# A decoder layer on one core: softmax sums as products of their own in the first group, one feed-forward tick moved in front of the output projection

## The chip, the cores and the metric

One core of a Trainium2 chip runs the whole program. The metric is the device time in microseconds (us), taken as the median of the runs shown. The engines are named as the profile names them: PE is TensorE (PEld its weight loads), DVE is VectorE, ACT is ScalarE, POOL is GpSimd, SP is the engine that issues most transfers.

## What is computed

The reference is one decoder layer over x (16 sequences of 128 tokens, 256 channels, fp32) and a context of 64 channels per token:

```
x = x + attn(layernorm(x))            # linear attention, 32 heads of 8, head norm, silu gate, Wo
x = x + xattn(layernorm(x), ctx)      # causal softmax attention, 16 heads of 16, Wout
x = x + ffn(layernorm(x))             # 8 experts (top 2), 176 hidden each, and a shared one of 704
```

The change touches the end of the second line, for each head

```
scores = q @ k.T / sqrt(16)           # causal mask
out    = softmax(scores) @ v          # = (exp(s - max) @ v) / sum(exp(s - max))
x      = x + out @ Wout.T
```

and the place of the work of the third line among that of the next group of sequences.

## The kernel before, in words

The 16 sequences go in four groups of four (g = 0 to 3; the title's "first group" is g = 0). A group goes through linear attention, then cross attention, then the output projection `Wout`, the residual and the third layer norm, and the router. Its feed-forward part is not done then: it is cut into 36 ticks (17 blocks of 128 hidden rows for each half of the tokens, and two to drain) and runs between the steps of the next group. The feed-forward of group 3 runs alone at the end.

A tick n is spread over the engines. PE makes the gate and up products of block n (L1018 to L1020, 12 matmuls of 256 columns, or 6 for the last block of a half, which has 64 rows) and the down products of block n - 2 (L1056 to L1058, 6 matmuls). ACT takes the silu (L774), DVE multiplies gate by up (L1469), POOL multiplies by the routing weight (L616), ACT makes the rounded high part (L764), POOL the low part (L605); the down products wait for that low part (`h_lo`). `COUNT` says how many ticks stand at which named point of a group's program: n0 to n5 up to the query projection, x0a to x3c in cross attention (b = 0 to 3 is the sequence), y0 in front of the output projection, r0 to r3 behind it. Every engine has its instructions in a fixed order written out by hand, and semaphores between engines.

Cross attention of a sequence b: scores and row maxima (DVE L1571), transposed exponentials (ACT L881), the causal cut (POOL L670), and `attend` (L1266): 16 matmuls that give, for 32 columns per head, 16 columns of values and 16 of ones, that is outputs and sums side by side. For one half of the heads the sums lie on the partitions on which the other half has its values, so ACT copies the bank twice with masks (`first_heads`, L890 and L891), DVE adds the other half (`second_heads`, L1584 and L1585), and then `attended` takes the reciprocal (L1590), swaps partitions within pairs (L1592) and multiplies (L1595), which releases `yT_ready`. Group 0 has two sets of score banks and runs two sequences at a time; matmuls on constants (`idle_product`, L988) stand between its `attend` calls. The output projection (`out_projection`, L1196) is in two halves, for sequences 0 and 1 and for 2 and 3; the second waits for the `yT_ready` of sequence 3. Then DVE adds the residual (L1638), takes the statistics, POOL the root (L548), DVE applies it (L1385), and PE turns the result (`turn_norm`, L979).

In the shadow of that the next group begins: its first layer norm is turned by PE (L979), copied by ACT (`mixed_input`, L724) and DVE (`input_differences`, L1411 to L1415); both copies wait for POOL to zero the edge column (`zero_edge`, L556). DVE mixes the inputs (L1423), and PE projects them (`project`, L1014).

## Time and profile before

| | us |
|---|---|
| median of 3 runs | 668.2 (667.42 to 668.63) |
| the profiled execution | 670.88 |
| its span, first to last instruction | 668.8 |
| PE busy in the span | 615.7 (92%) |
| DVE busy | 409.9 (61%) |
| POOL busy | 338.4 (51%) |
| ACT busy | 280.6 (42%) |
| mean granted clock of TensorE | 0.977 |

The profile has a page (busy time, waits, the chain that ended last) and the trace behind it can be asked for a stretch. The granted clock is a share of 2.4 GHz; 0.5 is its lower level, 1.2 GHz. PE is the engine that is nearly always busy, so the places where it stands idle, or runs at the lower clock, are what is to be read.

### The profile page before, as it was taken

The numbers are of one execution on the slowest core, as the hardware profiler recorded it, in microseconds if no ns is written. First come the engines' busy times: TensorE is split into PE (matmuls) and PEld (weight loads), VectorE is DVE, ScalarE is ACT, GpSimd is POOL, SyncE is SP. The second block draws the span as 40 slices with busy tenths as digits, with TensorE's granted clock in tenths as the row PEclk, the third lists the DMA queues.
The fourth block names the chain that finished last, engine by engine and source line by source line (L and its number), as shares of the span: only waits on it lengthen the run. The fifth ranks groups of instructions, "written<-read, shape, count | busy, mean of one in ns | idle before, by whom it ended". The sixth has DMA issues, their size and how long they took to land.

```text
span 668.8 us, 15291 instructions
## 1 busy us (share of the span) xinstructions
PE 615.7 (92%) x6184; PEld 486.1 (73%) x6184; DVE 409.9 (61%) x856; ACT 280.6 (42%) x640; POOL 338.4 (51%) x453
## 2 busy tenths in 40 slices
PE   7987978499999999799999999899999999999996
PEld 6444446354888889654797888764697889889996
DVE  6797789759643555778763555768863365652220
ACT  4956234042335655242324655233323666343332
POOL 6673155014355666324364765333364666518766
PEclk9989987699999999899999999899999999999999
DMA  8921000002031121002021111002011111104220
GB/s 191 355 61 33 1 1 2 0 1 65 26 84 28 39 62 42 14 16 66 11 84 42 38 56 41 21 16 65 10 48 35 43 44 60 22 27 132 69 70 17
DMA packets 41824, 34.08 MB, mean 51 GB/s; under 512 B 9901, under 2 KB 41206, under 8 KB 41754
## 3 DMA queue, kind: packets, MB, share of 16 engines
q1 hardware_dynamic: 39850, 31.27, 16.9%
q10 hardware_dynamic: 1904, 1.84, 0.8%
q8 instruction: 49, 0.80, 0.5%
q14 instruction: 21, 0.17, 0.1%
HBM read 30.92 MB, written 2.17 MB: 49 GB/s over the span
## 4 chain that ended last, share of the span: by engine, by line
PE 33%; DVE 25%; POOL 17%; ACT 11%; issue 11%; DMA 2%; ACTq 0%; POOLq 0%; DVEq 0%
PE bank L1014 6%; DVE A L1494 6%; DVE nm L1571 5%; POOL hb L616 5%; POOL A L691 3%; POOL hT_last L700 3%; POOL hT L605 3%; PE bank L1196 3%; PE bank L1123 2%; ACT A L881 2%; ACT L795 2%; PE bank L1112 2%; PE bank L1011 2%; PE bank L1213 2%; DVE hb L1469 2%
## 5 line engine op out<-in xcount | busy, mean ns | idle before, releaser
L605 POOL TENSOR_TENSOR hT<-hb,hT 128x256 fp32r<-128x256 f32 (+1 forms) x102 | 78.4, 769 | 75.6 <-ACT hT L764 75.6
L616 POOL TENSOR_TENSOR hb<-hb,cwb 128x256 f32<-128x256 f32 (+1 forms) x102 | 76.4, 749 | 75.5 <-DVE hb L1469 75.4
L1469 DVE TENSOR_TENSOR hb<-hb,bank 128x256 f32<-128x256 f32 (+1 forms) x102 | 42.7, 419 | 115.3 <-ACT hb L774 115.3
L764 ACT ACTIVATE hT<-hb 128x256 fp32r<-128x256 f32 (+1 forms) x102 | 42.4, 416 | 128.5 <-POOL hb L616 128.5
L1018 PE MATMUL bank<-xTf,wGh 128*128 128x256 f32 x272 | 83.4, 307 | 0.0
L1494 DVE TENSOR_TENSOR A<-bank,decay 128x512 f32<-128x512 f32 x128 | 77.5, 681 | 8.4 <-PE bank L1112 8.4
L1019 PE MATMUL bank<-xTf,wGh 128*128 128x256 f32 x272 | 76.7, 282 | 0.0
L1020 PE MATMUL bank<-xTf,wGl 128*128 128x256 f32 x272 | 76.6, 282 | 0.0
L1019 PE MATMUL bank<-xTf,wUh 128*128 128x256 f32 x256 | 72.2, 282 | 0.0
L1018 PE MATMUL bank<-xTf,wUh 128*128 128x256 f32 x256 | 72.1, 282 | 0.0
L1020 PE MATMUL bank<-xTf,wUl 128*128 128x256 f32 x256 | 72.1, 281 | 0.0
L570 POOL TENSOR_TENSOR A<-A,mcol 128x512 f32<-128x512 f32 x32 | 35.1, 1101 | 71.6 <-PE bank L1112 64.6
L1056 PE MATMUL bank<-wDh,hT 128*128 128x256 f32 (+1 forms) x204 | 59.8, 293 | 5.3 <-POOL hT L605 4.9
L1018 PEld LDWEIGHTS bank<-xTf,wGh 128*128 128x128 f32 x272 | 51.5, 189 | 8.9 <-issue 6.2
L1058 PE MATMUL bank<-wDh,hT 128*128 128x256 f32 (+1 forms) x204 | 57.1, 280 | 0.0
L1057 PE MATMUL bank<-wDl,hT 128*128 128x256 f32 (+1 forms) x204 | 57.1, 280 | 0.0
L774 ACT ACTIVATE hb<-bank 128x256 f32<-128x256 f32 (+1 forms) x102 | 38.1, 374 | 44.3 <-PE bank L1020 44.2
L1019 PEld LDWEIGHTS bank<-xTf,wGh 128*128 128x128 f32 x272 | 51.4, 189 | 0.2
L1020 PEld LDWEIGHTS bank<-xTf,wGl 128*128 128x128 f32 x272 | 51.2, 188 | 0.0
L1571 DVE TENSOR_REDUCE nm<-bank 128x16 f32<-128x2048 f32 x16 | 36.5, 2283 | 19.7 <-PE bank L1234 19.5
L1018 PEld LDWEIGHTS bank<-xTf,wUh 128*128 128x128 f32 x256 | 48.3, 189 | 0.0
L1019 PEld LDWEIGHTS bank<-xTf,wUh 128*128 128x128 f32 x256 | 48.2, 188 | 0.0
(217 smaller groups left out, 1436.2 us busy)
## 6 DMA issues: line engine op xcount, KB each, us to landing
cwb<-cw_rows SPq DMA_DIRECT2D x54, 128.0 KB, 3.0
A<-cw_rows SPq DMA_DIRECT2D x18, 128.0 KB, 3.2
A<-in_x SPq DMA_DIRECT2D x4, 512.0 KB, 4.2
res<-in_x SPq DMA_DIRECT2D x4, 512.0 KB, 4.3
out_x<-res SPq DMA_DIRECT2D x8, 256.0 KB, 2.4
rawG<-in_L_ffn_w_gate SPq DMA_DIRECT2D x2, 704.0 KB, 6.2
rawU<-in_L_ffn_w_up SPq DMA_DIRECT2D x2, 704.0 KB, 6.8
cwb<-cw_rows SPq DMA_DIRECT2D x12, 112.0 KB, 2.5
```

What stands on the lines that cost most here:

```text
L605: pool.tensor_tensor(hT[hr, c % 2, 1, :], hb[hr, c % 2, :], hT[hr, c % 2, 0, :].bitcast(F32), ALU.subtract).then_inc(h_lo, 1)
L616: pool.tensor_tensor(hb[hr, c % 2, :], hb[hr, c % 2, :], cwb[hr, c % CWS, :], ALU.mult).then_inc(h_scaled, 1)
L764: act.activation(hT[hidden(n), c % 2, 0, :], hb[hidden(n), c % 2, :], ACT.Copy).then_inc(h_hi, 1)
L1018: mm(out_ap, wh, xh, start=start, stop=False, skip_group_check=skip)
L1019: mm(out_ap, wh, xl, start=False, stop=False, skip_group_check=skip)
L1020: return mm(out_ap, wl, xh, start=False, stop=stop, skip_group_check=skip)
L1056: mm(o, hi[:, t], wDh[hr, j, :], start=(j == 0 and b == 0), stop=False, skip_group_check=True)
L1057: mm(o, hi[:, t], wDl[hr, j, :], start=False, stop=False, skip_group_check=True)
L1058: last = mm(o, lo[:, t], wDh[hr, j, :], start=False, stop=j == FB - 1, skip_group_check=True)
L1469: tt(h, h, up_part(PS[5 + c % 2], n), ALU.mult).then_inc(gu_used, 1)
L1494: tt(att[:, (u % 2) * 4 + i, :].rearrange("p (j t) -> p j t", j=4), PS[SCORE_BANKS[(4 * u + i) % 7]][:, :].rearrange("p (j t) -> p j t", j=4),
L1571: nc.vector.tensor_reduce(nm[:].rearrange("p (i h) -> p i h", i=4), PSB[:, score_base(g, b):score_base(g, b) + 4, :].rearrange("p i (h t) ...
```

## The change

In group 0 the kernel goes back to sums that are products of their own: `attend` there makes 32 matmuls of which 16 have a constant of ones and zeros (`onesp`, made by three more POOL instructions at the start) as weights, the halves of heads accumulate in one bank, and DVE's `attended` is a reciprocal read from the bank and a multiplication. ACT's copies, the two DVE additions, the swap and the `idle_product` calls between the `attend` calls go. The next group's first turn, its copy and its differences come after the last `attend` of group 0, the output projection of group 0 waits for all four sequences, and two of DVE's splittings of weights move from x2a to r2.

In groups 1 to 3 the arithmetic of `attend` is as before. `zero_edge` moves in front of the x3c ticks. One tick leaves n4 (2 to 1) and one is added at y0 (1 to 2), so that every tick from n5 to x3c is one number lower. On DVE the first y0 product stands in front of the normalisation of sequence 3 (`normalised`, the former `attended`) and the second behind it. `project(g + 1, 0)` moves in front of the down products of r2, and `mixed_input(g + 1, 1)` in front of r1 on DVE.

```diff
+        onesp = sb("onesp", [P, 2, 2 * XD], F32)
...
-        COUNT = dict(n0=1, n1=2, n2=2, n3=2, n4=2, n5=1, y0=1, r0=2, r1=1, r2=1, r3=1)
+        COUNT = dict(n0=1, n1=2, n2=2, n3=2, n4=1, n5=1, y0=2, r0=2, r1=1, r2=1, r3=1)
...
-        LOW_AT = dict(n5=(1, 2, 3), x0a=(0, 4, 5), x2a=(6, 7))
+        LOW_AT = dict(n5=(1, 2, 3), x0a=(0, 4, 5), r2=(6, 7))
...
+            made(pool.memset(onesp[:], 0.0))
+            for w in range(2):
+                made(pool.memset(onesp[:, w, XD * w:XD * w + XD], 1.0))
...
+                    if b == GB - 1 and g + 1 < NG:
+                        zero_edge(g + 1)
                     point(g, f"x{b}c")
 
-                if g + 1 < NG:
-                    zero_edge(g + 1)
                 point(g, "y0")
...
                         point(g, f"x{b}b")
-                        first_heads(b)
-                        if b == 2:
-                            mixed_input(1)
-                        first_heads(b + 1)
...
+                if g == 0:
+                    mixed_input(1)
                 point(g, "y0")
...
                     for m in range(2):
+                        for s in range(2):
+                            for w in range(2):
+                                for i in range(4):
+                                    v = xvp[:, b, 8 * m + 2 * i + w, :] if s == 0 else onesp[:, w, :]
+                                    a = (2 * s + m) * T
+                                    last = mm(PS[attend_bank(g, b)][32 * i:32 * i + 32, a:a + T], v, weights_of(g, b)[:, i, (2 * m + w) * T:(2 * m + w + 1) * T],
+                                              start=w == 0, stop=w == 1, skip_group_check=True)
...
                         attend(b)
-                        if b == 2:
-                            turn_norm(0, 1, tokx, 2)
-                        idle_product(10 - 2 * b, 1)
                         attend(b + 1)
...
+                if g == 0:
+                    turn_norm(0, 1, tokx, 2)
                 point(g, "y0")
-                if g == 0:
-                    pe.wait_ge(o_taken, 3)
-                out_projection(yT, [(yT_ready, g * 4 + 2), (yT_ready, g * 4 + 2)], wX[:, 1], (0, 1), wout_ready)
+                halves = 2 if g else 4
+                out_projection(yT, [(yT_ready, g * 4 + halves), (yT_ready, g * 4 + halves)], wX[:, 1], (0, 1), wout_ready)
...
                     down(g - 1, n - 2)
+                if g + 1 < NG:
+                    project(g + 1, 0)
                 point(g, "r2")
                 if g + 1 < NG:
-                    project(g + 1, 0)
                     point(g, "r3")
...
+                def attended(b):
+                    dve.wait_ge(o_part, g * 4 + b + 1)
+                    if b:
+                        dve.wait_ge(yT_ready, g * 4 + b)
+                    nc.vector.reciprocal(rec, PS[attend_bank(g, b)][:, 2 * P:4 * P]).then_inc(rec_ready, 1)
+                    dve.wait_ge(rec_ready, g * 4 + b + 1)
+                    tt(yT[:, :, b * T:(b + 1) * T], PS[attend_bank(g, b)][:, 0:2 * P].rearrange("p (m t) -> p m t", m=KC),
+                       rec.rearrange("p (m t) -> p m t", m=KC), ALU.mult).then_inc(yT_ready, 1)
...
-                point(g, "y0")
+                if g:
+                    ffn_tick(g - 1, ticks_at(g, "y0")[0])
+                    normalised(GB - 1)
+                    for n in ticks_at(g, "y0")[1:]:
+                        ffn_tick(g - 1, n)
+                else:
+                    input_differences(1)
...
+                if g + 1 < NG:
+                    mixed_input(g + 1, 1)
                 point(g, "r1")
                 if g + 1 < NG:
-                    for c in range(1, 4):
+                    for c in range(2, 4):
                         mixed_input(g + 1, c)
```

DVE before, at the end of group 1's cross attention: the last sequence's additions, reciprocal, swap and product, then the y0 tick's product (hb is the hidden block, A the activations) and the residual.

```order
L1584 SCALAR_TENSOR_TENSOR S<-bank,xcol,S 128x256 [waits o_copied]
L1585 SCALAR_TENSOR_TENSOR A<-bank,xcol,A 128x2x128
L1590 RECIPROCAL S<-S 128x256 [waits sums_ready]
L1592 STREAM_SHUFFLE S<-S 128x256 [waits rec_ready]
L1595 TENSOR_TENSOR A<-A,S 128x2x128 [waits o_taken,rec_swapped]
L1469 TENSOR_TENSOR hb<-hb,bank 128x256 [waits silu_done]
L1638 TENSOR_TENSOR res<-bank,res 128x512 [waits wout_ready]
```

DVE in the changed kernel, at the same place.

```order
L1603 SCALAR_TENSOR_TENSOR S<-bank,xcol,S 128x256 [waits o_copied]
L1604 SCALAR_TENSOR_TENSOR A<-bank,xcol,A 128x2x128
L1479 TENSOR_TENSOR hb<-hb,bank 128x256 [waits silu_done]
L1609 RECIPROCAL S<-S 128x256 [waits sums_ready]
L1611 STREAM_SHUFFLE S<-S 128x256 [waits rec_ready]
L1614 TENSOR_TENSOR A<-A,S 128x2x128 [waits o_taken,rec_swapped]
L1479 TENSOR_TENSOR hb<-hb,bank 128x256 [waits silu_done]
L1656 TENSOR_TENSOR res<-bank,res 128x512 [waits wout_ready]
```

One product of a tick now stands ahead of the reciprocal and the other behind the swap and the multiplication.

PE before, behind the turn of group 1's third norm: the end of the down products of r1, those of r2, the first projection of group 2 and the first of r3.

```order
L1056 MATMUL bank<-wDh,hT 128x256 [waits h_lo]
L1057 MATMUL bank<-wDl,hT 128x256
L1058 MATMUL bank<-wDh,hT 128x256
L1056 MATMUL bank<-wDh,hT 128x256
L1057 MATMUL bank<-wDl,hT 128x256
L1058 MATMUL bank<-wDh,hT 128x256
L1014 MATMUL bank<-A,wA 128x512 [waits xm_ready,o_taken]
L1014 MATMUL bank<-A,wA 128x512 [waits xm_ready] x3
L1056 MATMUL bank<-wDh,hT 128x256 [waits h_lo]
```

The six ahead of the projection here are those of r2. PE in the changed kernel, at the same place.

```order
L1057 MATMUL bank<-wDl,hT 128x256
L1058 MATMUL bank<-wDh,hT 128x256
L1014 MATMUL bank<-A,wA 128x512 [waits xm_ready,o_taken]
L1014 MATMUL bank<-A,wA 128x512 [waits xm_ready] x3
L1056 MATMUL bank<-wDh,hT 128x256 [waits h_lo]
L1057 MATMUL bank<-wDl,hT 128x256
L1058 MATMUL bank<-wDh,hT 128x256
L1056 MATMUL bank<-wDh,hT 128x256
L1057 MATMUL bank<-wDl,hT 128x256
L1058 MATMUL bank<-wDh,hT 128x256
L1056 MATMUL bank<-wDh,hT 128x256 [waits h_lo]
```

Now the projection follows the down products of r1, and those of r2 and r3 stand together behind it.

PE before, in group 0, at the first two `attend` calls (pexB holds the second sequence's exponentials).

```order
L1266 MATMUL bank<-A 32x128 x15
L988 MATMUL bank<-identb 128x512 x10
L1266 MATMUL bank<-pexB,A 32x128 [waits p_ready]
L1266 MATMUL bank<-pexB,A 32x128 x15
L1227 MATMUL bank<-maskS,identb 128x512 [waits o_taken,p_exp]
```

PE in the changed kernel, at the second of them.

```order
L1277 MATMUL bank<-A,onesp 32x128 x8
L1277 MATMUL bank<-pexB,A 32x128 [waits p_ready]
L1277 MATMUL bank<-pexB,A 32x128 x7
L1277 MATMUL bank<-pexB,onesp 32x128 x8
L1277 MATMUL bank<-pexB,A 32x128 x8
L1277 MATMUL bank<-pexB,onesp 32x128 x8
L1227 MATMUL bank<-maskS,identb 128x512 [waits yT_ready,p_exp]
```

The ten matmuls on constants are gone, 16 matmuls are added to each call, and the next scores wait for DVE's last product of the sequence before instead of its last addition.

## Rows read from the trace of the kernel before

**Rows 1.** The page: busy time of PE and the granted clock in 40 slices
```profile
PE 615.7 (92%) x6184; PEld 486.1 (73%) x6184; DVE 409.9 (61%) x856; ACT 280.6 (42%) x640; POOL 338.4 (51%) x453
...
PEclk9989987699999999899999999899999999999999
```
**Rows 2.** What PE waited for: us in total, times, longest
```profile
PE bank L1196 <- DVE A L1595: 11.8, 4, 4.9
```
**Rows 3.** Timeline of PE, end of groups 1, 2 and 3: start, us, instruction, idle before
```profile
272.71 3.68 PE L1196 MATMUL bank<-wX,A 128*128 128x256 f32 x8 [2.95 <-DVE A L1595]
...
426.64 3.57 PE L1196 MATMUL bank<-wX,A 128*128 128x256 f32 x8 [2.95 <-DVE A L1595]
...
576.50 1.99 PE L1196 MATMUL bank<-wX,A 128*128 128x256 f32 x8 [0.99 <-DVE A L1595]
```
**Rows 4.** Stretches there and of the last feed-forward: length, busy PE to POOL, clock
```profile
269.00:272.70 3.70, 0.76 (x4) 0.33 (x2) 3.62 (x8) 0.26 (x1) 0.80 (x1) 1.00 0.06 15
272.70:276.00 3.30, 3.29 (x9) 2.64 (x9) 1.89 (x6) 0.42 (x1) 1.45 (x2) 0.52 0.08 22
...
576.00:579.00 3.00, 2.50 (x14) 2.29 (x15) 2.82 (x8) 0.42 (x1) 1.47 (x2) 1.00 0.06 6
...
610.00:620.00 10.00, 10.00 (x87) 10.00 (x86) 2.11 (x5) 3.44 (x10) 8.61 (x14) 1.00 0.35 105
```
**Rows 5.** Timeline of DVE at the end of group 1's cross attention
```profile
267.36 0.69 DVE L1411 COPY A<-bank 128x512 f32<-128x512 f32 x1 [0.97 <-POOL A L556]
...
269.98 1.74 DVE L1590 RECIPROCAL S<-S 128x256 f32<-128x256 f32 x1
...
272.23 0.42 DVE L1595 TENSOR_TENSOR A<-A,S 128x256 f32<-128x256 f32 x1
272.57 0.41 DVE L1469 TENSOR_TENSOR hb<-hb,bank 128x256 f32<-128x256 f32 x1
```
**Rows 6.** One line's instructions: duration in ns, least, median, most
```profile
L1595 DVE TENSOR_TENSOR A<-A,S x14: 425/866/881, 96.3 to 576.0; 128x256 f32<-128x256 f32 x14
```
**Rows 7.** Timeline around n4 of group 1: second norm applied, turned
```profile
191.19 1.80 DVE L1385 TENSOR_SCALAR A<-res,mv,rstd 128x256 f32<-128x256 f32 x4
194.68 1.03 PE L979 MATMUL bank<-ident,A 128*128 128x128 f32 x8
```
**Rows 8.** Timeline behind the third norm of group 1, PE and POOL
```profile
281.22 1.04 PE L979 MATMUL bank<-ident,A 128*128 128x128 f32 x8
284.18 0.39 PE L1056 MATMUL bank<-wDh,hT 128*128 128x256 f32 x1 [1.21 <-POOL hT L605]
284.99 3.60 PE L1014 MATMUL bank<-A,wA 128*128 128x512 f32 x8
...
285.82 1.27 POOL L605 TENSOR_TENSOR hT<-hb,hT 64x256 fp32r<-64x256 f32 x1 [0.53 <-ACT hT L764]
```
**Rows 9.** Timeline of group 0's cross attention, PE, POOL and DVE
```profile
89.42 1.08 PE L1266 MATMUL bank<-A 128*32 128x128 f32 x32 [0.43 <-POOL A L670]
...
95.08 1.73 PE L1266 MATMUL bank<-pexB,A 128*32 128x128 f32 x32 [2.31 <-POOL pexB L670]
...
108.67 1.93 PE L1266 MATMUL bank<-A 128*32 128x128 f32 x32
...
109.44 3.30 POOL L670 TENSOR_SCALAR_AFFINE_SELECT pexB<-pexB 128x512 f32<-128x512 f32 x4 [1.35 <-ACT pexB L881]
...
121.64 3.78 PE L1196 MATMUL bank<-wX,A 128*128 128x256 f32 x8 [4.88 <-DVE A L1595]
...
125.45 0.69 DVE L1638 TENSOR_TENSOR res<-bank,res 128x512 f32<-128x512 f32 x1 [2.20 <-PE bank L1196]
```
**Rows 10.** A stretch of group 0, columns as in rows 4
```profile
95.00:99.00 4.00, 3.92 (x44) 2.13 (x48) 2.54 (x6) 0.84 (x2) 1.28 (x2) 0.57 0.00 0
```
**Rows 11.** Timeline of DVE in group 0: two splittings at x2a; idle at r2
```profile
110.86 2.15 DVE L1479 TENSOR_TENSOR wDl<-rawD,wDh 128x768 fp32r<-128x768 f32 x2
...
135.69 1.63 DVE L1423 SCALAR_TENSOR_TENSOR A<-A,cols 128x512 f32<-128x512 f32 x1 [2.15 <-PE bank L1014]
```

More of the change, by code:

```diff
@@ L150, in attend_bank, with attend_released @@
             return score_base(g, b) if g == 0 else 4
-        def sums_of(g, b):
-            return hb[:, 0, :] if g == 0 and b % 2 else rec
         SWAP = list(range(XD, 2 * XD)) + list(range(XD))
+        def attend_released(g, b):
+            return (o_taken, (g - 1) * 4 + b) if g else (yT_ready, b)
         tok2 = A[:, 5120:6144].rearrange("p (b c) -> p b c", b=GB)
```

71 lines of the change are left out of this document (33 added, 38 removed).

## The prediction

> **What bounds the kernel now.** I read the page first. PE is busy for 92% of the span and is at its full granted clock in nearly every slice [rows 1], so time can only come from the places where PE waits or runs at the lower clock. Next the list of what PE waited for: the longest entry is the output projection of cross attention, which waits for DVE's last multiplication (L1595) once per group, 11.8 us in four waits [rows 2]. Then the timeline at those four places. In groups 1 and 2 the second half of that projection waits 2.95 us, in group 3 it waits 0.99 us [rows 3], in group 0 4.88 us [rows 9]. The reader should see a second loss beside the wait: the same 8 matmul records take 3.68 and 3.57 us in groups 1 and 2 but 1.99 us in group 3 [rows 3]. The granted clock says why: in group 1 it is 1.00 over the wait and 0.52 over the 3.30 us behind it, that is nearly all at 1.2 GHz, while in group 3 after a wait of 0.99 us it is still 1.00 [rows 4]. PE's last piece is a wait of 1.21 us for POOL's low part behind the turn of the third norm [rows 8]; it stands in groups 1, 2 and 3 alike. Elsewhere in groups 1 to 3 PE has no wait that the change touches.
>
> **One more tick at y0, one less at n4.** PE's work is the same, only its place changes. A tick is 18 matmuls; over a stretch in which PE does nothing else 87 of them take 10.00 us, 0.115 us each [rows 4], so a tick is 2.07 us. In group 1 PE runs dry at 272.71 - 2.95 = 269.76; with a second tick ahead it does so at 271.83 on the clock of before. What it waits for is DVE's multiplication, which ends at 272.23 + 0.42 = 272.65 [rows 5]. Two edits move that end. The product of the y0 tick now stands in front of the reciprocal: plus 0.41. The edge column is zeroed before the x3c ticks and no longer after them: DVE's copy of the next group's turned input waited 0.97 us for it [rows 5], and everything behind on DVE, the reciprocal of 1.74 us too, comes 0.97 us earlier. So the end is at 272.65 - 0.97 + 0.41 = 272.09 and PE waits 0.26 us. The multiplication took from 0.425 to 0.881 us over its 14 records [rows 6], here 0.42; with POOL now busier beside it it may take 0.45 more, which makes 0.71 us. I take 0.4, between the two. If the edge brings nothing the wait is 1.2 to 1.7 us.
>
> With a wait of 0.4 us I expect no drop of the clock, because 0.99 us left it at 1.00 [rows 4]. Group 1 then saves 2.95 - 0.4 = 2.55 and 3.68 - 1.99 = 1.69, together 4.24 us; group 2 saves 2.55 and 3.57 - 1.99 = 1.58, together 4.13 us; group 3, whose wait of 0.99 is shorter than a tick, saves 0.99 us. **Sum 9.4 us.**
>
> DVE's order at this place puts the reciprocal behind a wait for ACT's silu of the y0 tick; who waits behind it is PE's second half. ACT makes that silu right after the copies that release DVE's additions, so I cost the wait at nothing beyond the 0.41.
>
> The multiplication's two lengths have a rule in the Trainium skill, in SBUF — State Buffer, § Who interferes with whom: a DVE instruction with two SBUF inputs contends with a GpSimd instruction that reads SBUF. By that rule the longer value holds wherever POOL works beside it, and the waits of groups 1 and 2 would be 0.71 us, which makes the sum 0.6 us smaller; by the row taken alone (0.42 at this place) it would be 0.3 us larger.
>
> The tick taken from n4 was cover for the second norm. DVE has applied it at 191.19 + 1.80 = 192.99; PE turned it from 194.68 on [rows 7]. One tick earlier is 192.61, with the last of four sequences needed some 0.77 us later, at 193.38. That is 0.39 us after it is there, so the removal costs nothing; if DVE is late by more than that, PE loses the difference, at most 2.07 us per group. The other ticks, with their 64-row block, their residual addition and SP's transfers of routing rows and of the next x, become one number lower at each point; the engines pass them on in the same rhythm, so I cost that at 0, with a bound of 0.3 us per group either way.
>
> **Down products of r2 behind the projection.** PE waits 1.21 us for the low part [rows 8] and then projects for 3.60 us; in the new order the projection comes first and hides the wait. That is in groups 1 and 2; in group 3 there is no next group and the wait stays. What is late next is the low part of the last block: POOL ends it at 285.82 + 1.27 = 287.09, 5.87 us after the turn began. PE reaches it after the turn and the down products of r1 (282.97, or 1.75 us after that beginning), 3.60 us of projection and 6 matmuls of 0.115, that is at 6.04 us, so it is there by 0.2 us. **2 x 1.21 = 2.4 us**, with 0 as the other bound. The projection needs the second mixed input, which DVE now makes ahead of r1 where it would wait for ACT.
>
> **Group 0.** Each `attend` doubles. The second one ran while the clock was low (95 to 99 us: 0.57 [rows 10]) and took 1.73 us [rows 9], so what follows comes up to 1.73 us later; the scores behind it run partly at the recovered clock and I take 1.5. The ten products on constants had ended 2.31 us before that call and give nothing back. The last `attend` could start when POOL's cut was done, 109.44 + 3.30 = 112.74 [rows 9]; now at 114.24. It takes 2 x 1.08 = 2.16 at the full clock (116.4). DVE's chain behind it is one reciprocal of 1.74 and one multiplication of 0.42, and 0.1 for the handing over (118.7): ACT's copies, the additions, the swap and the three steps of input differences are no longer in it. A reciprocal from a bank is not in the trace; the multiplication's spread bounds what it may add, 0 to 0.45. Then both halves of the projection, 2 x 1.99 less their overlap, 3.9 us: 122.6 against 125.45 before, when DVE added the second half [rows 9]. **Gain 2.9 us.** Bounds: if the first shift does not reach the end, 4.4; if PE stays at the lower clock throughout (no filler products keep it busy now, 1.93 us per 16 matmuls as in one row of rows 9, the projection 2 x 3.78), the end is at 114.24 + 3.86 + 2.26 + 7.56 = 127.9, a loss of 2.5. I take the full clock because PE's work there becomes denser, not sparser. The two splittings, 2.15 us, leave x2a and fall at r2 into an idle stretch of DVE of 2.15 us [rows 11]: 0, or at most a few tenths. The three memsets at the start lie ahead of a root for which POOL waits: 0.
>
> **Sum.** 9.4 + 2.4 + 2.9 = 14.7 us. The profiled execution took 670.88 (span 668.8 and 2.1 around it) and would take 656.2, span 654.1. The median of the runs shown is 668.2, 2.7 below that execution, and the prediction is made for it: 668.2 - 14.7 = **653.5 us**.
>
> **Rivals.**
> 1. Group 0 falls to the lower clock once its fillers are gone. For it: the clock was low there in one stretch even with them [rows 10]. Against: 32 matmuls per call. Time 653.5 + 2.9 + 2.5 = 658.9. Chance 0.12.
> 2. The wait at r2 only moves to the last low part at r3, for which I have 0.2 us: 653.5 + 2.4 = 655.9. Chance 0.08.
> 3. The cover at n4 is missed: DVE's second norm comes late by a tick in three groups. 653.5 + 3 x 2.07 = 659.7. Against: 0.39 us of slack on the row. Chance 0.06.
> 4. The added tick does not cover: its own down products or the silu in front of the reciprocal wait, PE still stands over 1.7 us in groups 1 and 2 and the clock falls as before. 653.5 + 2 x (1.3 + 1.6) = 659.3. This is also the case in which the change does not do what it says. Chance 0.06.
> 5. Slower than before: after the sparse end of group 0 the clock does not come back, and the projections of group 1's inputs, four of 3.60 us, run at 1.2 GHz. That adds 14.4 to rival 1: 673.3. It decides if PE's work from the turn of the third norm on does not lift the clock, which it did before. Chance 0.03.
>
> **How the numbers follow.** The forecast, 651 to 656, has 0.62. The rest, 0.03, is what I don't see. The best sum is 4.4 + 9.4 + 0.8 + 2.4 = 17.0, or 651.2; I set the low end at 650.8. The high end has to take in rivals 1 to 4, so 660.0; rival 5, and two of them at once, are left out, about 0.12. A measurement of this kernel can tell about 0.2% from no change, 1.3 us. Faster has all cases but rival 5 and what I don't see: 0.94; same 0.02; slower 0.04.
>
> **What the changed profile would show.** In groups 1 and 2 two ticks ahead of the output projection, its second half without a wait over 1 us and about 2 us long, the granted clock there 1.00. No wait of PE behind the r1 down products of groups 1 and 2, and one of 1.21 still in group 3. No wait at the turn of the second norm. Group 0's second addition of the residual near 122.6 us instead of 125.45. It would be wrong if the clock at y0 still reads near 0.5, or if the gap reappears at n4 or r3.

## The result and the profile after

The changed kernel takes **650.7 us** (median of 4 runs, 649.97 to 653.28) against 668.4 us (4 runs, 667.42 to 670.11) for the kernel before: ratio **0.9734**, 95% interval 0.9703 to 0.9766. The forecast was 653.5 us with a range of 650.8 to 660.0. The gain is 17.7 us where 14.7 were worked out, so the measured time lies 0.1 us below the low end of the range.

The profiled execution of the changed kernel has a span of 651.6 us, that of before 668.8. The first rows to read are again PE's busy share and the granted clock of the page, which answer to [rows 1]:

```profile
PE 608.5 (93%) x6296; PEld 484.9 (74%) x6296; DVE 409.7 (63%) x840; ACT 277.4 (43%) x632; POOL 337.5 (52%) x456
...
PEclk9989998799999999999999999999999999999999
```

PE has 112 instructions more (128 for the sums of group 0, less the 16 products on constants between its attends) and is busy for 7.2 us less. The slices with an 8 in the middle of the row, one behind each output projection of groups 1 and 2, are gone; only group 0 still shows lower ones.

The list of what PE waited for, to be set against [rows 2]:

```profile
PE bank L979 <- DVE A L1395: 4.0, 1, 4.0
PE bank L1277 <- POOL pexB L674: 3.7, 1, 3.7
PE bank L1056 <- POOL hT L609: 3.0, 8, 1.2
...
PE bank L1196 <- DVE A L1597: 1.7, 1, 1.7
...
PE bank L1196 <- DVE A L1614: 0.4, 2, 0.2
```

The entry of 11.8 us in four waits has become 1.7 us in group 0 and twice 0.2 in groups 1 and 2. The two longest that are left, 4.0 and 3.7 us, are both in group 0, where no feed-forward of a group ahead fills PE.

PE's timeline at the output projection of groups 1, 2 and 3 answers to [rows 3]:

```profile
263.99 1.89 PE L1196 MATMUL bank<-wX,A 128*128 128x256 f32 x8
266.09 1.99 PE L1196 MATMUL bank<-wX,A 128*128 128x256 f32 x8 [0.21 <-DVE A L1614]
...
413.97 1.99 PE L1196 MATMUL bank<-wX,A 128*128 128x256 f32 x8 [0.21 <-DVE A L1614]
...
557.88 3.62 PE L1196 MATMUL bank<-wX,A 128*128 128x256 f32 x16
```

The second half waits 0.21 us where it waited 2.95, takes 1.99 us where it took 3.68 and 3.57, and in group 3 both halves run in one piece. The stretches of group 1 (length, busy time of PE, PEld, DVE, ACT and POOL, granted clock, DMA share, GB/s), as in [rows 4]:

```profile
266.00:268.10 2.10, 2.01 (x10) 1.80 (x11) 1.97 (x7) 0.42 (x1) 1.12 (x2) 1.00 0.10 29
268.10:271.40 3.30, 3.30 (x30) 3.30 (x30) 3.03 (x9) 0.39 (x1) 1.57 (x3) 1.00 0.07 22
```

The clock is 1.00 (2.4 GHz) where it was 0.52, which is 1.2 GHz nearly throughout. DVE there, as in [rows 5]:

```profile
260.26 0.68 DVE L1421 COPY A<-bank 128x512 f32<-128x512 f32 x1
...
263.03 0.40 DVE L1479 TENSOR_TENSOR hb<-hb,bank 128x256 f32<-128x256 f32 x1
263.36 1.74 DVE L1609 RECIPROCAL S<-S 128x256 f32<-128x256 f32 x1
...
265.61 0.42 DVE L1614 TENSOR_TENSOR A<-A,S 128x256 f32<-128x256 f32 x1
```

The copy that waited 0.97 us for the edge waits for nothing, the y0 tick's product stands in front of the reciprocal, and the last multiplication takes 0.42 us. PE behind the third norm of group 1, as in [rows 8]:

```profile
272.92 1.04 PE L979 MATMUL bank<-ident,A 128*128 128x128 f32 x8
...
274.51 3.60 PE L1014 MATMUL bank<-A,wA 128*128 128x512 f32 x8
...
279.65 1.06 PE L1330 MATMUL bank<-xTf,wR 128*10 128x128 f32 x32
```

No wait stands between the turn and the router's product (L1330, which is L1320 before); the one of 1.21 us is gone in groups 1 and 2, and group 3 still has it, at 569.29.

**Where the time came from.** The start of the router's product marks each group well, since nothing but group 0 differs ahead of the first. It stood at 135.58, 289.41, 443.24 and 587.64 us and stands at 131.62, 279.65, 427.52 and 570.65. Cut further at the first half of the output projection and at the turn of the third norm, the 17.2 us between the two spans divide so:

| stretch | forecast | measured |
|---|---|---|
| group 0, up to its router product | 2.9 | 3.96 |
| projection to third norm's turn: groups 1, 2, 3 | 4.24, 4.13, 0.99 | 4.42, 4.31, 1.26 |
| turn to router product: groups 1, 2 | 1.21, 1.21 | 1.46, 1.47 |
| all else (cover at n4, shifted ticks, tail) | 0 | 0.3 |
| sum | 14.7 | 17.2 |

**A second thing is needed to read the times.** The profiled execution of the changed kernel is 3.3 us above the lowest of the other three. The further kernels below point to the reason: their profiled executions differ in the granted clock of the first 40 us, and in nearly all of them group 0 goes with it (start of the router product of group 0, us):

| clock of 0:40 | group 0 as before | group 0 as changed | gain |
|---|---|---|---|
| 1.00 | 132.96 and 132.97 (fill_gap, rest_only) | 128.44 to 128.50 (tick_back, order_back, split_back) | 4.5 |
| 0.97 | 135.58 (before) | 131.62, 131.46, 131.41 (after, edge_back, proj_back) | 4.0 to 4.2 |
| 0.91, 0.92 | none | 134.18, 134.37 (after_again, g0_only) | |

The mean over those 40 us isn't the whole of it. fill_norm below, whose only edit lies behind the output projection of group 0, starts that projection at 116.95 with a clock of 0.92; after_again does so at 120.01 with 0.91, and the changed kernel at 117.05 with 0.97. Two kernels below that edit the new group 0 itself, g0_fillers and pow_late, have their router products at 128.77 and 129.15 with a clock of 1.00.

Behind that product two executions of the changed kernel agree to 0.1 us (519.98 and 519.92 us from there to the end). The forecast took 2.7 us off the profiled execution for the median. A likely cause lies here: the profile of before is of the second row, while most of the timed executions of both kernels have times that fit the first. Only one execution of each kernel is profiled, so this isn't shown. Row against row the gain is 4.5 + 13.2 = 17.7 us, which is what the medians say.

### The profile page after: what moved, and what is told of

Same layout as the page of the kernel before. It is cut to its first block, busy times and chain, and to the rows that moved or that the text cites. A ratio compares the mean times of both kernels' runs of the same rounds, so it can differ in the third digit from the quotient of the medians.

```text
span 651.6 us, 15490 instructions
## 1 busy us (share of the span) xinstructions
PE 608.5 (93%) x6296; PEld 484.9 (74%) x6296; DVE 409.7 (63%) x840; ACT 277.4 (43%) x632; POOL 337.5 (52%) x456
## 3 DMA queue, kind: packets, MB, share of 16 engines
q1 hardware_dynamic: 39850, 31.27, 17.2%
## 4 chain that ended last, share of the span: by engine, by line
PE 36%; DVE 23%; POOL 17%; ACT 11%; issue 10%; DMA 2%; ACTq 0%; SPq 0%; POOLq 0%; DVEq 0%
PE bank L1014 7%; DVE A L1504 6%; DVE nm L1581 5%; POOL hb L620 4%; POOL A L695 3%; POOL hT_last L704 3%; PE bank L1196 3%; POOL hT L609 3%; ACT A L885 2%; PE bank L1123 2%; ACT L799 2%; PE bank L1011 2%; PE bank L1213 2%; PE bank L1112 2%; DVE hb L1479 2%
```

## The experiments

Medians therefore move by up to 3 us with the mixture of starts. I read each kernel by its **steps**, from one router product to the next in its profiled execution (before 153.83, 153.83, 144.40 and a tail of 81.16; after 148.03, 147.87, 143.13, 80.95), and give the times beside them. In tick_back and proj_back the tail, which no edit touches, is 3.0 us longer, and in order_back 1.2 us (82.15). It is left out of the steps, but the times have it. The difference is the clock's. In all 16 profiled executions PE waits about 1.2 us and then 0.2 to 0.4 us around the router product of group 3; in these three it then runs at 1.2 GHz for 3 to 7 us (proj_back 0.50 to 0.51 from 574 to 580 us), in the other thirteen the product runs at the full clock. The same product in proj_back and in the changed kernel:

```profile
573.07 1.89 PE L1329 MATMUL bank<-xTf,wR 128*10 128x128 f32 x32 [0.39 <-DVE xTf L1672]
```

```profile
570.65 1.06 PE L1330 MATMUL bank<-xTf,wR 128*10 128x128 f32 x32 [0.39 <-DVE xTf L1675]
```

### Group 0 alone, and the rest alone

g0_only is the changed kernel with the counts of ticks, the edge, the order at r2 and DVE's order at y0 of groups 1 to 3 as before. rest_only is the kernel before with only those edits.

```
 g0_only, against the changed kernel:
-COUNT = dict(..., n4=1, n5=1, y0=2, ...)
+COUNT = dict(..., n4=2, n5=1, y0=1, ...)
...
-                if g + 1 < NG:
-                    project(g + 1, 0)
-                point(g, "r2")
+                point(g, "r2")
+                if g + 1 < NG:
+                    project(g + 1, 0)
```

> The kernel before with the group 0 part of the change alone; COUNT, the edge and the order in groups 1 to 3 are as before. Theory (the parts add): the router products of group 0 start 4.0 us earlier, as in the changed kernel (131.62 instead of 135.58), nothing else moves, and the span goes from 668.8 to 664.8. Rival (the parts help each other, say by a clock that stays up): the distance from those products to the end also shrinks by over 1 us and the span is below 663.8.

Measured: 662.35 us (661.01 to 668.20, ratio 0.9909, 0.9871 to 0.9947), steps 153.56, 153.37, 144.31, 80.89.

> The kernel before with the tick, the edge, the order on DVE and the projection in front of r2 changed in groups 1 to 3, group 0 as before. Theory (the parts add): group 0 to its router products as before (135.58), groups 1, 2 and 3 shorter by 5.8, 6.0 and 1.3 us, span about 655.6. Rival: part of the gain in groups 1 to 3 came from the new group 0 (the projections of group 1 start at another clock), then the span is over 656.6.

Measured: 655.70 us (654.87 to 660.52, ratio 0.9805, 0.9738 to 0.9871), steps 147.88, 147.91, 143.12, 80.92, each within 0.15 us of the changed kernel's. rest_only alone takes all 13.2 us of groups 1 to 3 (13.4 from its router product of group 0 to the end), so the new group 0 has no part in them. By the medians the two kernels gain 6.1 and 12.8 us over the kernel before (668.49 beside them), 18.9 together, where the whole change gains 17.7: the halves add up, but for 1.1 us that g0_only also gains in later steps. Those are the clock's. With the same wait of 2.94 us ahead of it, the second half in group 1 takes 3.10 us where it took 3.68, at a clock of 0.62 against 0.52, and once the wait is gone there is nothing of this kind to gain. g0_only's router product is at 134.37, not the expected 131.62, since its start is of the third row.

### One edit undone at a time

**The tick.** `COUNT` alone back to `n4=2, y0=1`.

> The changed kernel with the tick put back from y0 to n4. Theory (the tick only covers a wait): PE waits 0.21 + 2.07 = 2.3 us for DVE's last multiplication in groups 1 and 2 and about 1.4 in group 3; if the granted clock stays at 1.00 after 2.3 us the span is 651.6 + 4.1 + 1.4 = 657.1; if it falls as it did behind 2.95 us, another 1.6 us in each of groups 1 and 2, 660.3. Rival (the tick taken from n4 opened a wait there which going back closes): less than 655.

Measured: 656.46, 656.63, 662.49 and 668.21 us (ratio 0.9832, 0.9751 to 0.9913), steps 151.66, 151.61, 145.15: 3.63, 3.74 and 2.02 us more, 9.4 together. PE's second halves in groups 1, 2 and 3, and the clock over the first and second:

```profile
265.01 2.51 PE L1196 MATMUL bank<-wX,A 128*128 128x256 f32 x8 [2.37 <-DVE A L1614]
...
416.48 3.68 PE L1196 MATMUL bank<-wX,A 128*128 128x256 f32 x8 [2.34 <-DVE A L1614]
...
565.73 1.99 PE L1196 MATMUL bank<-wX,A 128*128 128x256 f32 x8 [1.79 <-DVE A L1614]
```

```profile
265.00:267.40 2.40, 2.39 (x9) 1.99 (x10) 1.55 (x5) 0.00 (x0) 0.00 (x0) 0.78 0.02 6
267.40:270.00 2.60, 2.60 (x15) 2.60 (x14) 1.86 (x6) 0.00 (x0) 0.40 (x1) 0.55 0.00 0
416.40:419.00 2.60, 2.52 (x6) 2.07 (x7) 1.63 (x6) 0.00 (x0) 0.00 (x0) 0.52 0.02 8
```

The cover of the tick is 2.16 us of the wait, and the clock falls behind waits of 2.37 and 2.34 us, not behind 1.79. Both of my expected outcomes seem to occur. Two executions at a mean clock of 0.988 took 656.5 and 656.6 us, which is about 650.2 plus the waits alone (2.3, 2.3 and 2.0); they have no trace. The profiled one, at 0.978, took 662.5: 9.4 us more for the steps and 3.0 for the tail. The fourth, 668.2 at 0.970, is left aside. Even with the edge and DVE's order improved, the tick is what the gain at y0 rests on.

**The down products at r2.** `point(g, "r2")` ahead of the projection again.

> The changed kernel with the projection behind the down products of r2 again and the second mixed input behind r1. Theory: the wait for POOL's low part is back at 1.21 us in groups 1 and 2, span 651.6 + 2.4 = 654.0. Rival (the wait was also paid at the last low part, or the earlier mixed input matters by itself): a difference of less than 1.2 or over 3.6 us.

Measured: 657.35 us (652.87 to 658.73, ratio 0.9792, 0.9715 to 0.9869), steps 149.41 and 149.25, 1.38 us more each. The wait is back word for word:

```profile
275.58 0.39 PE L1056 MATMUL bank<-wDh,hT 128*128 128x256 f32 x1 [1.21 <-POOL hT L609]
```

It costs 1.38 us and not 1.21, because a wait also takes away the overlap of the products on both sides of it: where nothing waits, a record of 256 columns lasts 0.28 us and the next one starts 0.12 us behind it. The time (657.35) is higher than the expected 654.0 by more than that; the profiled execution has the long tail, and the lowest one took 652.9.

**The edge.** `zero_edge` behind the x3c ticks again in groups 1 to 3.

> The changed kernel with the edge column zeroed behind the x3c ticks again in groups 1 and 2. Theory: DVE's chain is 0.97 us later there, PE waits 0.21 + 0.97 = 1.2 us instead of 0.21, the clock stays at 1.00 and the span is 651.6 + 1.9 = 653.5. Rival: the added tick alone is cover enough, because other work of DVE fills the gap, and the span is within 0.5 us of 651.6.

Measured: 654.54 us (652.20 to 654.62, ratio 0.9741, 0.9676 to 0.9805), steps 148.87 and 148.69, 0.84 and 0.82 us more. DVE's copy, and PE ahead of and in the projection:

```profile
261.11 0.69 DVE L1423 COPY A<-bank 128x512 f32<-128x512 f32 x1 [0.97 <-POOL A L560]
```

```profile
263.66 0.39 PE L1058 MATMUL bank<-wDh,hT 128*128 128x256 f32 x1 [0.46 <-POOL hT L609]
...
266.79 1.99 PE L1198 MATMUL bank<-wX,A 128*128 128x256 f32 x8 [0.43 <-DVE A L1616]
```

DVE pays the 0.97 us as expected, but PE's wait at the projection is 0.43, not the expected 1.2: the same delay already reached PE some 3 us earlier, through the tick's product, POOL's low part and 0.46 us at the down products, and what PE waits there it needn't wait again. The price of the edge is about right (0.8 of 0.97), its place was not.

**DVE's order.** The multiplication of the last sequence ahead of the first y0 tick's product.

```
-                    ffn_tick(g - 1, ticks_at(g, "y0")[0])
-                    normalised(GB - 1)
-                    for n in ticks_at(g, "y0")[1:]:
+                    normalised(GB - 1)
+                    for n in ticks_at(g, "y0"):
                         ffn_tick(g - 1, n)
```

> The changed kernel with both y0 products on DVE behind the normalisation of sequence 3. Theory: the wait of PE for the last multiplication goes (0.21 us in groups 1 and 2), since 0.41 us leave DVE's chain, but the block's low part comes over 2 us later; the down products that need it stand four matmul groups behind and have the room: span 651.2. Rival: the late product holds the gate and up bank or the low part, PE waits at r0: span over 652.6.

Measured: 654.87 us (652.86 to 660.89, ratio 0.9772, 0.9702 to 0.9842), steps 149.36, 149.20, 143.89, that is 1.33, 1.33 and 0.76 us **more**. As expected the output projection then has no wait at all, and yet the group is slower:

```profile
260.78 3.76 PE L1196 MATMUL bank<-wX,A 128*128 128x256 f32 x16
...
270.31 1.08 PE L979 MATMUL bank<-ident,A 128*128 128x128 f32 x6 [0.63 <-DVE A L1395]
271.69 0.44 PE L979 MATMUL bank<-ident,A 128*128 128x128 f32 x2 [0.29 <-DVE A L1395]
```

The tick's product is made at 262.41, behind the reciprocal, 2.6 us later than in its turn; POOL's and ACT's steps of that tick and of the one behind it come late, the second product on DVE too, and the additions and the norm behind that. PE meets it at the turn of the third norm. The wait of 0.21 us that is left in the changed kernel is the cheaper one.

### The clock by itself

fill_gap is the kernel before with products on constants between the two halves of the output projection, twelve in groups 1 and 2, three in group 3. They compute nothing and shorten no wait.

```
+                        if q and g and done is wout_ready:
+                            idle_product(12 if g + 1 < NG else 3, 1)
                         for k in range(KC):
```

> The kernel before with matmuls on constants (12 in groups 1 and 2, 3 in group 3) in the gap between the two halves of cross attention's output projection; the wait itself stays. Theory (1.6 us of each loss is the lower clock, which follows the idle of PE): the second half takes about 2.0 us instead of 3.68 and 3.57, granted clock 1.00, span 668.8 - 3.4 = 665.4. Rival (the second half was long for another reason, such as a bank or operands that arrive late): no change, 668.8.

Measured: 664.96 us (663.84 to 669.59, ratio 0.9934, 0.9900 to 0.9969), steps 152.10, 151.93, 144.30, 80.91: 1.73 and 1.90 us less in groups 1 and 2.

```profile
266.93 2.75 PE L988 MATMUL bank<-identb 128*128 128x512 bf16 x12
270.03 1.99 PE L1198 MATMUL bank<-wX,A 128*128 128x256 f32 x8 [0.34 <-DVE A L1597]
```

The second half takes 1.99 us though DVE is exactly as late as before. So the 1.69 and 1.58 us that the prediction read from [rows 3] were the clock's alone, and what lowers the clock is that PE stands idle, not that DVE is late.

### Group 0

**Products on constants between the attends** of the changed kernel, ten behind the first and six behind the third: `idle_product(10 - 2 * b, 3)`.

> The changed kernel with the products on constants put back between the attend calls of group 0, 10 and 6 (in another bank). Theory: they hold nothing up, as the clock fell at 95 us with them too; behind the third attend call they stand in front of the fourth, which comes 0.4 to 1.3 us later: span 652 to 653. Rival (they keep the clock up): attend takes 2.2 us each, group 0 is shorter by 1 us or more, span below 650.6.

Measured: 651.63 us (650.71 to 652.76, ratio 0.9710, 0.9656 to 0.9763). The clock is 1.00 from 95 to 120 us, and nothing comes earlier: the first router product is at 128.77, 0.3 later than at the same start without them, of which 0.2 lie ahead of the first attend. The last attend starts at 110.37, after the constants, though POOL's cut was done at 109.69. What the clock gives back the constants take.

**POOL's power behind the second sequence's cuts** in group 0, to shorten the wait of 3.70 us ahead of the second attend: `if b == (0 if g else 1) and g + 1 < NG`.

> The changed kernel, but in group 0 POOL raises the variances of the next group's first norm to the power behind the causal cuts of the second sequence, not between those of the first and the second. It is POOL's 2.31 us at 89.40 us, ahead of the cuts for which PE waits 3.70 us before the second attend (95.01 us). My theory: the two attends of group 0 are then 2.3 us closer, the wait is 1.4 us, and everything to group 0's output projection comes 2.3 us earlier, since PE's chain through scores, maxima and attends has POOL's cuts in it only at this place; 650.7 - 2.3 = 648.4 us. Rival: the exponentials of the third and fourth sequence, on ACT, or POOL's later pieces set the pace of the last two attends, the last attend starts at 112.2 as before, and the time stays at 650.7. A third: a shorter wait moves where the low clock falls, plus or minus 1.5 us.

Measured: 654.50 us (649.17 to 656.06, ratio 0.9751, 0.9713 to 0.9789). No gain: the wait ahead of the second attend is 1.37 us, but it is 1.36 as well in the executions with this start that leave the power where it was. POOL shows why:

```profile
90.14 4.20 POOL L674 TENSOR_SCALAR_AFFINE_SELECT pexB<-pexB 128x512 f32<-128x512 f32 x4 [1.39 <-ACT pexB L885]
94.31 1.00 POOL L552 TENSOR_TENSOR rstd<-ve,mhalf 128x4 f32<-128x4 f32 x1
```

The cuts begin 0.76 us behind the start of the first attend, where they began 1.68 us behind it in order_back, but they take 4.20 us where they took 3.27. What stretches them is DVE's splitting of weights: the first two of the four, beside it, take 1.72 and 1.35 us, the last two 0.63 each.

```profile
90.15 2.52 DVE L1489 TENSOR_TENSOR wDl<-rawD,wDh 128x1024 fp32r<-128x1024 f32 x2
```

ACT doesn't set the end: its last exponentials are done at 91.55, the last cut at 94.34. The kernel with both edits, below, has the other start, where the wait was 3.70 us. There ACT is done at 93.48, the cuts begin 1.98 us earlier than in after_again (92.07 for 94.05) and end at the same time, and the wait is still 3.56 us:

```profile
92.07 5.20 POOL L674 TENSOR_SCALAR_AFFINE_SELECT pexB<-pexB 128x512 f32<-128x512 f32 x4 [0.31 <-ACT pexB L885]
```

My theory falls. The first rival is right that nothing is gained, though not for its reason: without the power the cuts only run longer beside DVE's splittings. Whether moving those would give something back here is not tested.

**Products on constants ahead of the turn of the third norm**, seventeen of 512 columns, in group 0, where PE stands 4.04 us: `if g == 0: idle_product(17, 7)`.

> The changed kernel with 17 products on constants (512 columns each, into bank 7) in group 0 between the output projection and the turn of the third norm, where PE stands 4.04 us and the turn of 1.97 us and the projection of 5.12 us behind it run at a low clock (0.54 from 125 to 130 us). They leave no wait shorter: DVE's norm ends at the same time. My theory: what is lost there is the clock, so the turn takes 1.04 and the projection 3.6 us, and the router product starts 2.4 us earlier, 650.7 - 2.4 = 648.3 us. Rival: the products on constants don't hold the clock (as the ten at the start of group 0 did not keep it at 95 to 99 us), and the time is 650.7 or, if they run at half clock and end behind the norm, up to 3 us more.

Measured: 650.50 us (649.08 to 654.54, ratio 0.9712, 0.9677 to 0.9748), beside 653.26 for the changed kernel on the same chip.

```profile
120.50 3.83 PE L988 MATMUL bank<-identb 128*128 128x512 bf16 x17
124.70 1.41 PE L979 MATMUL bank<-ident,A 128*128 128x128 f32 x8 [0.37 <-DVE A L1397]
125.95 3.60 PE L1014 MATMUL bank<-A,wA 128*128 128x512 f32 x8
```

From the projection to the router product are 12.52 us; the changed kernel has 14.17 to 14.57. That is 1.7 to 2.0 us less, of which the later steps lose 0.3 again. The expected 2.4 was a little too much, because the turn takes 1.41 and not 1.04 us. By the times alone the two kernels can't be told apart: the intervals overlap.

**Both** of the last two:

> Both edits in one kernel: the power behind the second sequence's cuts, and the 17 products on constants ahead of the turn of the third norm, both in group 0 alone. If they are independent 650.7 - 2.3 - 2.4 = 646.0 us; if the second only regains a clock that the first lets fall elsewhere, 648.3.

Measured: 652.67 us (648.12 to 654.88, ratio 0.9729, 0.9689 to 0.9768); its stretch from projection to router product is again short, 12.53 us. It has the lowest single execution of all, but its median is no better.

**The changed kernel again**, as a measure of all this:

> The changed kernel itself once more, beside the three below on the same chip: the measure of what one execution differs from the next. Profiled steps from router product to router product 148.0, 147.9, 143.1 and a tail of 81.0 us, the first router product at 128.5 or 131.6 us after the start of the span, 128.5 if the granted clock of the first 40 us is 1.00 and 131.6 if it is 0.97. Median 650.7 us, executions between 649.5 and 653.5. If the spread of the runs so far comes from the edits and not from the executions, all of these are within 1 us of each other.

Measured: 653.26 us (650.17 to 655.97, ratio 0.9746, 0.9711 to 0.9781), steps 148.03, 147.90, 143.13, 80.86. The router product of group 0 was at 134.18, a start that I had not listed. Between the two profiled executions of this kernel the spread is of group 0 alone. These six executions have a median 2.6 us above that of the first four, with nothing changed.

**DVE's two splittings.** split_back is the changed kernel with them at x2a again, split_late the kernel before with them at r2 and nothing else:

```
-LOW_AT = dict(n5=(1, 2, 3), x0a=(0, 4, 5), x2a=(6, 7))
+LOW_AT = dict(n5=(1, 2, 3), x0a=(0, 4, 5), r2=(6, 7))
```

> The changed kernel with the two splittings of DVE (1.07 us each, two inputs in SBUF) back from r2 to x2a of group 0, beside POOL's last cuts. Theory: they are what made POOL's four cuts of the fourth sequence 3.30 us before and 2.40 us in the changed kernel, since DVE and POOL then read SBUF at once; the cuts take 3.2 to 3.4 us again, end after PE is done with the third sequence's products, and the last attend starts 0.3 to 0.6 us later than 3.24 us behind the third. The router product of group 0 is then 0.3 to 0.6 us later than the changed kernel's for the same clock in the first 40 us (128.5 at 1.00, 131.5 at 0.97, 134.2 at 0.91): 650.7 + 0.4 = 651.1 us. Rival: the cuts take 2.40 us as they do now, and it was the copies and additions for the partner rows, not the splittings, that stretched them; the router product stays within 0.1 us.

Measured: 651.17 us (649.96 to 656.08, ratio 0.9734, 0.9677 to 0.9792), router product at 128.44.

> The kernel before with the two splittings moved from x2a to r2 as in the change and nothing else. Theory: POOL's cuts of the fourth sequence take 2.4 to 2.6 us where they took 3.30, and DVE's additions of the third sequence's partner rows start up to 1.4 us earlier (they stood behind the splittings until 112.94 us), so the output projection's second half of group 0 starts 0.8 to 1.4 us earlier and the router product at 131.6 to 132.2 (clock 1.00 in the first 40 us; before 132.97) or 134.2 to 134.8 (clock 0.97; before 135.58): 668.4 - 1.1 = 667.3 us. Rival: the ten products on constants and the last attend set the pace there, the splittings were hidden, and the time is that of before, 668.4; at r2 they may even cost 0.3.

Measured: 667.69 us (666.97 to 670.47, ratio 0.9957, 0.9930 to 0.9983). The second half of group 0's projection starts 30.82 us behind the first attend, 1.40 us earlier than before (32.22), as expected. The router product is only 0.56 us earlier behind it, because the stretch from the turn of the third norm to it takes 6.96 us instead of 6.13, at a lower clock (0.67 over the projection of the next group against 0.79). POOL's last cuts in the two kernels:

```profile
106.15 3.19 POOL L674 TENSOR_SCALAR_AFFINE_SELECT pexB<-pexB 128x512 f32<-128x512 f32 x4 [0.27 <-ACT pexB L885]
```

```profile
109.78 2.59 POOL L670 TENSOR_SCALAR_AFFINE_SELECT pexB<-pexB 128x512 f32<-128x512 f32 x4 [1.34 <-ACT pexB L881]
```

The splittings stretch the cuts: 3.19 us with them and 2.40 without in the changed kernel, 3.30 with and 2.59 without in the old one. But in the changed kernel that costs nothing (128.44 against 128.45 and 128.50), since the third sequence's doubled attend lasts just as long. In the old one the last attend starts at 112.66 instead of 113.75, but not because of the cuts: PE has no wait there in either execution, and its third attend and the turn behind it take less because the full clock is back sooner (the turn 1.09 us for 1.97). What the splittings give the old kernel is DVE's: its additions of the third sequence start at 111.94 and no longer at 112.94, behind them.

## Why the prediction came out 3 us too high

Of the 3.0 us, 1.6 are group 0's (4.5 at the start of the first row, for 2.9) and 1.4 lie behind it (13.2 for 11.8). Of those 1.4, 0.36 are the wait at y0 that was put at 0.4 us and not 0.21, 0.78 the overlap that three waits took away, and 0.3 the rest of the table. That the median came to lie 0.1 us outside the range is chance: the six further executions of the same kernel have a median of 653.3, inside it. The group 0 step is off at both starts that can be compared.

**The tick, the edge, the order at y0: right, and right in size.** Worked out was a wait of 0.26 us at the clock of before; 0.21 was measured, where I took 0.4. fill_gap shows that the slow second half was the clock alone, tick_back that the tick is needed. Measured were 9.99 us instead of 9.4: 0.2 more each in groups 1 and 2 from the wait, and 0.3 in group 3, where a wait of 0.99 us gave 1.26 when it went.

The sentences on the multiplication's two lengths can be judged. At the place that matters L1614 takes 0.42 us with no POOL work beside it, so the shorter value held. Elsewhere the trace agrees with the rule of the Trainium skill (SBUF — State Buffer, § Who interferes with whom). Beside POOL's cuts the same multiplication takes 0.86 to 0.87 us in six of its twelve records, and in the other three, one in each group, six times as long as alone:

```profile
222.49 2.64 DVE L1614 TENSOR_TENSOR A<-A,S 128x256 f32<-128x256 f32 x1
```

```profile
222.45 2.40 POOL L674 TENSOR_SCALAR_AFFINE_SELECT A<-A 128x512 f32<-128x512 f32 x4
```

PE doesn't wait for it there.

**DVE's wait for the silu, costed at nothing: right,** and order_back shows the reverse, that the other order costs 1.33 us. I had weighed what the product delays behind it, but not what is delayed if the product itself comes late.

**The tick taken from n4: right.** PE has no wait at the turn of the second norm, and the stretch from router product to output projection is unchanged to 0.2 us in all three groups.

**The down products at r2: right, and a little small.** 1.46 us a group instead of 1.21, confirmed from the other side by proj_back (1.38). No wait took its place at r3. The term that was mis-sized is the wait itself: it was counted as long as the timeline shows it, without the overlap.

**Group 0: the step that failed.** Forecast 2.9 us, measured 4.0 in the profiled execution and 4.5 at the start of the first row. The step is "now at 114.24" for the start of the last attend. The rows of the last two attends (in pieces of 16) and of POOL's cut:

```profile
108.92 0.93 PE L1277 MATMUL bank<-A 128*32 128x128 f32 x16 [0.48 <-POOL A L674]
...
112.16 0.82 PE L1277 MATMUL bank<-pexB,A 128*32 128x128 f32 x16
...
117.05 3.72 PE L1196 MATMUL bank<-wX,A 128*128 128x256 f32 x16 [1.74 <-DVE A L1597]
```

```profile
109.13 2.40 POOL L674 TENSOR_SCALAR_AFFINE_SELECT pexB<-pexB 128x512 f32<-128x512 f32 x4 [0.27 <-ACT pexB L885]
```

It started at 112.16, 2.08 us earlier. I had taken the end of POOL's cut of before, 112.74, and added 1.5 us for the second attend, which doubles. That attend did take 1.5 us more (3.23 for 1.73), but the delay didn't reach the end. It was 0.83 us at DVE's maxima behind it (100.77 for 99.94), because the scores between ran at the full clock sooner (the first four masks took 1.38 us for 1.89). At the transposed scores' product ahead of the last exponentials it turned round, the first row before, the second now:

```profile
106.72 2.02 PE L1253 MATMUL bank<-A 32*128 32x128 f32 x32
```

```profile
107.32 1.11 PE L1253 MATMUL bank<-A 32*128 32x128 f32 x32
```

The clock was 0.50 there before (106 to 112 us) and is 1.00 until 109 now. So ACT began the exponentials at 108.47 for 108.77, and POOL the cut at 109.13 for 109.44. The prediction had this as its better bound ("if the first shift does not reach the end, 4.4") and not as its sum. It is no steady gain: the product takes 2.02 us in the four profiled executions with the old group 0, 1.11 or 1.12 us in nine with the new one, and 2.02 or 2.03 us in after_again, g0_only and both, whose output projections start 3 us later than those of the second row.

Two more things differ. The cut took 2.40 us and not 3.30, 0.7 to 0.8 of it by DVE's splittings, which I had costed at 0 for DVE and had not looked at for POOL (split_back, split_late). So it ended at 111.53. And the last attend no longer waits for the cut, but for PE's own third attend, which with its sums takes 3.24 us from 108.92, mostly at the lower clock. That the changed kernel takes the same time with the splittings back beside the cut shows that the bound had passed to PE, and that the shift and not the cut's length is the step that cost the forecast its time. From the last attend on the working held: 8.36 us forecast to the second addition of the residual, 8.64 measured, at 120.80 instead of 122.6. A reciprocal from a bank takes 1.76 us where one from SBUF takes 1.74.

The addition is 4.65 us earlier than before, and 0.7 of that are lost again behind it, which I hadn't considered. PE stands 4.04 us for the norm and turns it in 1.97 us, as before, but from there to the router product it then takes 5.06 us where it took 4.37, at a clock of 0.69 against 0.79. fill_norm, with the constants in that wait, has a turn of 1.41 and a projection of 3.60 us.

**The rivals.** Rival 1, a lower clock in group 0, came true for single pieces and not for the sum. Rivals 2, 3, 4 and 5 did not occur. The fault of the range is its low end. It was the best case of each term as I had sized it, and the terms lacked the overlap that goes with each wait, some 0.26 us in three places.

**What stays open:** what sets the clock of the first 40 us, and where in group 0 the low clock falls, in one execution and not in another; why the waits at group 3's router product lowered the clock in three executions and not in thirteen; and why in g0_only and split_late the second halves behind a wait of 2.94 us took 2.7 to 3.1 us instead of 3.6. What each edit of group 0 brings by itself was measured only for the products on constants and the splittings, and the earlier second mixed input was undone only together with the projection.

## What to carry to other kernels

Before a wait is taken away, ask what the clock did behind it: here a wait of 2.95 us cost 4.6, and fillers that compute nothing gave back 1.7 to 1.9 of it. When a longer piece is said to delay all that follows, go along the chain and see where the delay is taken up: here one product at the other clock took up 0.9 us. Cost an edit that moves work off one engine also for the engine that ran beside it, and ask whether the bound is still the same engine once both have moved. And compare executions stretch by stretch between fixed points: 1 us in one stage was plain there, while the medians moved by 3 us with what happened in the first 40.

## What the runs showed of the hardware

- The granted clock over the first 40 us (1.00, 0.97 or 0.91, among others) differs from execution to execution of one kernel, and mostly with it the place at which the low clock falls in the next 90: on the first attend (3.64 us for its 64 products in order_back) or on the second (3.23 in the changed kernel). fill_norm has it on the first with a clock of 0.92. Between executions of the same group 0 the end of it moved by up to 5.7 us and the steps behind it by 0.1. Here are three executions with the same group 0, order_back, the changed kernel and its repetition, over the start:

```profile
0.00:40.00 40.00, 33.23 (x210) 21.33 (x214) 30.05 (x65) 25.75 (x70) 29.03 (x59) 1.00 0.89 253
```

```profile
0.00:40.00 40.00, 33.46 (x194) 21.13 (x198) 29.51 (x64) 25.68 (x69) 29.18 (x59) 0.97 0.88 253
```

```profile
0.00:40.00 40.00, 33.05 (x170) 22.53 (x174) 30.54 (x62) 25.57 (x69) 27.91 (x59) 0.91 0.90 253
```

- Behind idle times of PE of 0.21, 0.43, 0.99 and 1.79 us in an otherwise full stretch the clock stayed at 2.4 GHz; behind 2.34, 2.37 and 2.95 us the profiled executions show it at 1.2 GHz for most of the next 3 us (0.55, 0.52 and 0.52 over 2.6 to 3.3 us). Two unprofiled executions of tick_back, at a mean clock of 0.988, seem to have escaped it. Where two waits stand close together, 1.2 and 0.2 to 0.4 us at the router product of group 3, the clock fell to 0.50 in three of 16 profiled executions and cost the tail 1.2 to 3.0 us.
- A wait of PE that the timeline shows as 0.99 or 1.21 us costs 1.26 and 1.38 to 1.47: a product of 256 columns is shown for 0.28 us and the next one starts 0.12 us behind it, and a gap takes that overlap away.
- A DVE multiplication of 128x256 with both inputs in SBUF takes 0.42 us alone. Beside POOL's four cuts of a 128x512 tile it takes 0.86 to 0.88 us, and the cuts 2.59, or it takes 2.62 to 2.64, and the cuts 2.40. Beside DVE's splittings of weights the cuts take 3.2 to 3.3 us, and 4.20 and 5.20 in the two kernels in which they start early into them.
